# Self and cross attention of a decoder layer: values on packed weights, four value buffers, fewer waits and fewer written-out slots on TensorE

## The reference

```
def _L0_attn_ref(x, w_qkv, w_proj, b_proj):              # self attention
    qkv = einsum('bnc,cd->bnd', x, w_qkv).reshape(b, n, 3, H, HD).transpose(2, 0, 3, 1, 4)
    attn = softmax(einsum('bhnd,bhmd->bhnm', q * scale, k), axis=-1)
    out = einsum('bhnm,bhmd->bhnd', attn, v).transpose(0, 2, 1, 3).reshape(b, n, c)
    return einsum('bnc,cd->bnd', out, w_proj) + b_proj
x = _layernorm(x + _L0_attn_ref(x, ...))
x = _layernorm(x + _L0_xattn_ref(x, ctx_1024, ctx_1024, ...))   # same shape, keys and values of the context, causal
x = _layernorm(x + _L0_ffn_ref(x, ...))
x = _layernorm(x + _L1_attn_ref(x, ...))                 # differential attention, heads of 64
x = _layernorm(x + _L1_xattn_ref(ctx_1024, x, mask, ...))
x = _layernorm(x + _L1_ffn_ref(x, ...))                  # mixture of experts
```

## Time and profile before

| what | value |
|---|---|
| runs | 1548.01, 1548.19, 1548.48 us; median 1548.19 us |
| profiled execution | 1543.35 us, of it span 1541.6 us |
| busy share of the span | PE 96%, PEld 82%, DVE 81%, ACT 59%, POOL 45% |
| first layer's attention | 0 to 271 us: self items in a loop 42 to 120, written slots 120 to 160, cross items in a loop 160 to 250 |
| feed-forward, differential attention, latent attention, experts | 271 to 340, 340 to 930, 930 to 1435, to the end |
| TensorE's granted clock, mean | 0.992 of full speed |

### The profile page before, as it was taken

How to read it: one execution, slowest core, us unless ns; L and a number is a source line. 1 busy time by engine, 2 the same in 40 slices (tenths; PEclk the granted TensorE clock), 3 DMA queues, 4 the chain that set the end, 5 groups by cost and what they waited for, 6 DMA issues and landing times. The chain is left out here.

```text
span 1541.6 us, 79105 instructions
## 1 busy us (share of the span) xinstructions
PE 1486.4 (96%) x31480; PEld 1267.9 (82%) x31480; DVE 1251.3 (81%) x3574; ACT 911.8 (59%) x2620; POOL 692.9 (45%) x1140
## 2 busy tenths in 40 slices
PE   7999999998999999999999998999999999999796
PEld 5887888886777787787877786999999999999664
DVE  7998888687878888888878885688888888888655
ACT  5888888544555555555555554666666666666242
POOL 4789777212433333333333333344444444444347
PEclk9999999999999999999999999999999999999898
DMA  4215222112210011111111011121212121212231
GB/s 116 72 54 148 72 65 64 49 53 62 62 41 27 27 29 29 27 29 32 31 28 27 27 31 28 52 58 57 63 48 65 46 65 46 65 46 63 75 110 56
DMA packets 157679, 82.70 MB, mean 54 GB/s; under 512 B 17641, under 2 KB 153115, under 8 KB 157568
## 3 DMA queue, kind: packets, MB, share of 16 engines
q1 hardware_dynamic: 154800, 77.68, 18.2%
q0 software_dynamic: 2048, 3.15, 0.6%
q10 hardware_dynamic: 720, 0.33, 0.1%
HBM read 61.03 MB, written 21.27 MB: 53 GB/s over the span
## 5 line engine op out<-in xcount | busy, mean ns | idle before, releaser
L1527 PE MATMUL bank<-diff_xT,diff_w_score 128*32 128x128 f32 x8192 | 249.0, 273 | 3.3 <-ACT diff_keys L1647 1.8
L1527 PEld LDWEIGHTS bank<-diff_xT,diff_w_score 128*32 128x32 f32 x8192 | 220.6, 110 | 34.5 <-ACT diff_keys L1647 13.8
L2150 ACT ACTIVATE lat_prob<-bank,lat_neg_max 128x128 f32<-128x128 f32 x512 | 180.6, 367 | 75.9 <-DVE lat_neg_max L2269 75.6
L2375 POOL TENSOR_TENSOR lat_prob<-lat_prob,lat_inv_sum 128x512 f32<-128x512 f32 x128 | 133.4, 1042 | 198.1 <-DVE lat_inv_sum L2297 197.1
L1860 POOL TENSOR_TENSOR diff_prob<-diff_prob,diff_inv_sum 128x512 f32<-128x512 f32 x64 | 67.1, 1049 | 325.4 <-DVE diff_inv_sum L1762 325.4
L1647 ACT ACTIVATE diff_keys<-bank 128x512 f32<-128x512 f32 x256 | 151.7, 595 | 67.6 <-PE bank L1527 66.6
L2070 PE MATMUL bank<-lat_catT,lat_query 128*128 128x128 f32 x1024 | 138.4, 278 | 2.3 <-ACT lat_query L2161 2.1
L2039 PE MATMUL bank<-lat_catT,lat_w_score 128*128 128x128 f32 x1024 | 135.4, 275 | 0.6 <-ACT lat_catT L2142 0.6
L2059 PE MATMUL bank<-lat_w_vo,lat_ctxT 128*128 128x128 f32 x1024 | 132.6, 278 | 1.1 <-ACT lat_ctxT L2173 1.1
L2070 PEld LDWEIGHTS bank<-lat_catT,lat_query 128*128 128x128 f32 x1024 | 124.5, 192 | 4.7 <-ACT lat_query L2161 3.7
L2039 PEld LDWEIGHTS bank<-lat_catT,lat_w_score 128*128 128x128 f32 x1024 | 124.6, 192 | 1.2 <-ACT lat_catT L2142 0.8
(11 more groups left out here) (273 smaller groups left out, 3611.1 us busy)
## 6 DMA issues: line engine op xcount, KB each, us to landing
lat_c_rep<-cat SPq DMA_DIRECT2D x128, 128.0 KB, 2.6
stage<-low_y SPq DMA_DIRECT2D x64, 64.0 KB, 1.6
diff_x_rep<-stage SPq DMA_DIRECT2D x128, 32.0 KB, 1.7
lat_c_t<-cat SPq DMA_DIRECT2D x32, 128.0 KB, 2.2
exp_w<-in_L_ffn_w_dram SPq DMA_DIRECT2D x16, 256.0 KB
expert_rows<-latw_zeros SPq DMA_DIRECT2D x4, 548.0 KB, 5.9
exp_rows<-expert_rows SPq DMA_DIRECT2D x8, 274.0 KB
low_x_t<-in_x_dram SPq DMA_DIRECT2D x32, 64.0 KB, 1.9
```

The costliest lines, as they stand in the source:

```text
L1527: last = nc.tensor.matmul(ring[(k + d) % 2][at, j * P:(j + 1) * P], w_score[:, H1 * (k // 2) + HS * d + 4 * (k % 2) + j, at], xT[:, :], st ...
L2150: last = nc.scalar.activation(prob[:, q, m, :], ps_s[q][:, m * T:(m + 1) * T], ACT.Exp, bias=neg_max[:, q, m:m + 1], accum_out=row_sum[:, ...
L2375: nc.gpsimd.tensor_tensor(prob[:, q, :, :], prob[:, q, :, :], inv_sum[:, q, :, None].to_broadcast([P, 4, T]), ALU.mult)\
```

## The change

- `wv` becomes 64 columns wide: the weights of the even or odd heads lie packed. L379 then has 64 moving columns, and its result lies in 64 columns of PSUM per sequence. The clearing of `wv` and its semaphore go.
- `v_blk` gets four buffers in place of two, all of it cleared once. ScalarE copies the values of the even heads from partitions 0 to 63 and those of the odd heads from partitions 64 to 127, 64x128 each, in place of one 128x256; the zeros of the other half stay from the clearing. `v_ready` counts two per item. ScalarE no longer waits for L394 of the slot (`av_done`) before this copy.
- Seven waits of TensorE's slot go, each implied by another: `onorm_done` and `oT_ready` ahead of L394, the first of its `pT_ready`, `xT_ready` (from slot 2 on) and `pT_ready` ahead of L406, `xT_ready` (from slot 2 on) and `qT_ready` ahead of L418.
- TensorE gets its own program shape in `LowHeads`: slots -2 to 5 written out, 6 to 29 looped, 30 to 33 written out, 34 to 61 looped, 62 to 66 written out. `self.quarter` tells each slot which of the four value buffers it uses. In the differential attention TensorE writes out pairs 0 and 1, loops over 2 to 30 and writes out 31 to 33.

```diff
-        self.wv = sb("wv", [P, 2, 2, P])
+        self.wv = sb("wv", [P, 2, 2, S])
-        self.v_blk = sb("v_blk", [P, 2, 2, H0 // 2, VW])
+        self.v_blk = sb("v_blk", [P, 4, 2, H0 // 2, VW])
...
     def tensor(self, pe, between=None):
-                        last = nc.tensor.matmul(ps_v[L * n:L * (n + 1), b * P:(b + 1) * P],
+                        last = nc.tensor.matmul(ps_v[L * n:L * (n + 1), b * S:(b + 1) * S],
                                                 self.xT[:, par, int(cr(0)), at:at + L], self.wv[:, int(cr(0)), odd, :],
                                                 start=True, stop=True)
...
-                wait(pe, self.onorm_done, i - 2)
-                wait(pe, self.oT_ready, i - 2)
...
-                    if hp % 4 == 0:
+                    if hp == 4 or hp == 0 and not on(0):
                         wait(pe, self.pT_ready, 2 * i - 3 + hp // 4)
...
-                wait(pe, self.xT_ready, i + 2)
-                wait(pe, self.pT_ready, 2 * i - 2)
+                if isinstance(i, int) and i < 2:
+                    wait(pe, self.xT_ready, i + 2)
...
-                wait(pe, self.xT_ready, i + 2)
-                wait(pe, self.qT_ready, i + 1)
+                if isinstance(i, int) and i < 2:
+                    wait(pe, self.xT_ready, i + 2)
...
-                wait(pe, self.v_ready, i + 1 if on(0) else NI)
+                wait(pe, self.v_ready, 2 * i + 2 if on(0) else 2 * NI)
...
-        self.slots(pe, slot, between)
+        for i in range(-2, 6):
+            written(i)
+        with pe.Fori(1, NPAIR // 4 - 1) as q:
+            for m in range(4):
+                self.quarter = (m + 2) % 4
+                slot(4 * q + m + 2, 2 * q + m // 2 + 1, m % 2, lambda d: True, lambda d: False)
+        for i in range(NPAIR - 2, NPAIR + 2):
+            written(i)
+        with pe.Fori(NPAIR // 4, NI // 4 - 1) as q:
+            for m in range(4):
+                self.quarter = (m + 2) % 4
+                slot(4 * q + m + 2, 2 * q + m // 2 + 1, m % 2, lambda d: True, lambda d: True)
+        for i in range(NI - 2, NI + 3):
+            written(i)
+            between(i)
...
     def scalar(self, act, between=None):
                 wait(act, self.v_done, i + 2)
-                wait(act, self.av_done, i)
...
-                nc.scalar.activation(self.v_blk[:, 1 - par, :, :, 0:2 * HD0],
-                                     ps_v[:, 0:2 * P].rearrange("p (b g e) -> p b g e", b=2, e=2 * HD0),
-                                     ACT.Copy).then_inc(self.v_ready, 1)
+                for odd in range(2):
+                    at = slice(odd * S, (odd + 1) * S)
+                    nc.scalar.activation(self.v_blk[at, (self.quarter + 1) % 4, :, :, odd * HD0:(odd + 1) * HD0],
+                                         ps_v[at, 0:P].rearrange("p (b g e) -> p b g e", b=2, e=HD0),
+                                         ACT.Copy).then_inc(self.v_ready, 1)
...
     def vector(self, dve, between=None):
-        nc.vector.memset(self.wv[:, :, :, :], 0.0).then_inc(self.wv_zeroed, 1)
         both = self.v_blk[:, :, :, :, :].rearrange("p n b g e -> p (n b g) e")
-        nc.vector.memset(both[:, :, 2 * HD0:VW], 0.0).then_inc(self.ones_done, 1)
+        nc.vector.memset(both, 0.0).then_inc(self.ones_done, 1)
...
-            pairs(pe, pair)
+            for i in range(2):
+                pair(i)
+            with pe.Fori(2, NPAIR - 1) as i:
+                pair(i)
+            for i in range(NPAIR - 1, NPAIR + 2):
+                pair(i)
```

More of the change, by code:

```diff
@@ L262, in written @@
         def written(i):
+            self.quarter = i % 4
             slot(i, i // 2, i % 2, lambda d: 0 <= i + d < NI, lambda d: i + d >= NPAIR)
@@ L270, in slots @@
             for m in range(4):
+                self.quarter = m
                 slot(4 * q + m, 2 * q + m // 2, m % 2, lambda d: True, lambda d: False)
@@ L393, in slot @@
                         at = slice(L * n, L * (n + 1))
[L394 removed]
+                        last = nc.tensor.matmul(ps_o[at, hp, :], self.probT[:, hp, at], self.v_blk[:, (self.quarter + 2) % 4, n // 2, hp, :],
                                                 start=True, stop=True)
@@ L440, in slot, with written @@
                 cross_weights()
+        def written(i):
+            self.quarter = i % 4
+            slot(i, i // 2, i % 2, lambda d: 0 <= i + d < NI, lambda d: i + d >= NPAIR)
         pe.wait_ge(self.consts.ident_done, 1)
-        self.slots(pe, slot, between)
+        for i in range(-2, 6):
[13 more added lines that the diff above has]
+            between(i)
     def scalar(self, act, between=None):
```

7 lines of the change are left out of this document (2 added, 5 removed).

## The result

The changed kernel takes 1539.71 us (median; 1537.22 to 1541.24) against 1548.19 for the kernel before, now over more runs (1545.61 to 1550.3). The ratio is 0.9942, with an interval of 0.9931 to 0.9952: 7.4 to 10.7 us off. The forecast was 1541.7 us, 6.5 us off. The profiled execution takes 1537.97 us where that of before took 1543.35, so the two profiles differ by 5.4 us only. The medians differ by 3.1 us more than the profiles; that, too, has to be explained.

What follows compares the result with a forecast made beforehand. TensorE was taken to bound the first layer's loops, VectorE close behind in the self loop. Cross loop 5.3 plus self loop 1.2 gave 6.5 us off, 1548.19 to 1541.7 us; range 1538.5 to 1546.0.

Steps and rivals of the forecast that it cites:

- The value matmuls: First layer's L379: 64 columns in place of 128 shorten the segment from 0.46 to 0.24 us, saving 0.22 per slot.
- rival D: Value matmuls don't shorten as said, issue or weight loads setting their pace; 0.06 us per slot or less; chance 0.07.
- The cross loop: First layer's cross-attention slots, about 24: TensorE is the bound, so all 0.22 us per slot counts, 5.3 us saved.
- The self loop: First layer's 20 self-attention slots: VectorE's 3.62 us floor leaves 0.06 per slot, also after back edges; 1.2 us saved.
- ScalarE's copies: Copy into v_blk in two: 0.34 us in place of 0.28, bounds 0 to +0.28 more, covered by 0.35 idle.
- The waits at nothing: Seven implied TensorE waits removed: issued under running matmuls, so costed at nothing; at most 0.1 us per slot more.
- the loops' shape at nothing within 1 us: TensorE's new looped and written slots and pairs: taken as zero, from -1 to +1 us.
- Rival E: Slower: loop bodies don't stay in TensorE's instruction store, or jumps stall the ring; 1554.7 us at 1.0 per back edge; chance 0.08.
- From profile to median: Whole kernel: the median's 4.8 us above the profiled execution carried over unchanged, from 1536.9 to 1541.7 us.
- B: TensorE gives more: L394 shrinks too, by 0.1 us, cross period 3.69; 1537.5 to 1540.7 us; chance 0.16.
- C: Another ring of VectorE, ScalarE and TensorE takes most of the gain; 1543.7 to 1547.5 us; chance 0.14.
- A: The forecast itself: 4.5 to 7.5 us saved, cross loop 3.79 us a slot, 1540.7 to 1543.7 us; chance 0.55.

Runs made afterwards that it cites:

- e6: Kernel before with the values part and the seven TensorE waits gone, TensorE's program shape as before: 1550.3 us, 1.0001 of the kernel before.
- e12: Changed kernel with only the differential attention's TensorE program shape turned back (pairs 0 to 3 and 30 to 33 written out): 1540.88 us, 0.9947 of the kernel before.

## Why the prediction was right, and where only its sum was

The time, 1539.71 us, lies in the range and 2.0 us below the forecast. By its steps:

*The value matmuls: right.* 0.24 us was forecast for the segment, 0.25 was measured; it is the same with the values alone. 16 matmuls in 0.25 us are 15.6 ns each. The rule of the Trainium skill, "TensorE: Matmul & The Clock Gate", Back-to-back issue gap, that matmuls start no closer than about 25 ns, thus doesn't hold here, where they lie in four column groups, and rival D falls.

*The cross loop: right.* 0.22 us per slot over 22 slots, 4.84 us; the kernels with the values all lie between 83.71 and 84.23 us there, but for the one with a stop of 1.54 us in that stretch (e6, 86.61). Forecast for 24 slots: 5.3.

*The self loop: three times too high.* Forecast 1.2 us, measured: five groups of four slots at 14.78 against 14.85 us give 0.35. The plain slots shrank as forecast, to VectorE's floor. The step that failed is "because the jump is common to both": the idle time after a back edge was read as partly TensorE's, because the trace named L394. It stays at 0.28 though L394 is now over before the statistics end, so it doesn't wait for TensorE; it is VectorE's own, as the forecast's lower bound for those slots had it (nothing gained there). Besides, the slot that holds it grew: 14.85 - 3 x 3.68 = 3.81 us before, 14.78 - 3 x 3.60 = 3.98 after. VectorE's waits from 42 to 120 us, after the change, show where the rest went, with 0.2 us in the second row before:

```profile
DVE low_inv_sum L567 <- DVE low_stats L594: 1.2, 4, 0.3
DVE low_o_norm L575 <- DVE low_inv_sum L567: 1.2, 5, 0.4
```

The 1.0 us more over five groups is 0.2 each, about the slot's growth of 0.17. What makes VectorE wait for its own reciprocal there wasn't tried.

*ScalarE's copies: wrong, and covered.* Forecast 0.34, with bounds up to 0.56; measured 0.59, above the upper bound. The row taken, a 128x128 copy at 0.17, was the wrong one: a copy of 64 partitions is not cheaper than one of 128 with twice the columns (0.28). It fits, because the 0.35 idle plus the old copy's 0.28 make 0.63. The floor worked out for ScalarE was wrong as well: with the measured copies it gives 4.01 - 0.35 + 0.31 = 3.97 us, and the slot runs at 3.80, so not everything between two waits was work that can't move closer. ScalarE is now busy 79.36 of 85 us in the cross stretch, as VectorE is (79.67), and the two are next in line.

*The waits at nothing, the loops' shape at nothing within 1 us: wrong as rules, right in their sum here.* Alone the removed waits cost 5.7 us, and with the other parts in place they gained some 3. Alone the shapes gave nothing, and with values and waits they gave 9. What was missing is a cost that the profile of before doesn't show at all: TensorE stops of up to 2.3 us where the program passes through code that is fetched, at a packet's edge. Written slots hold such places, and 21 fewer packets mean fewer of them. Rival E looked at the right resource but on the wrong side: back edges, a second pass of code that is already there, cost TensorE next to nothing (the cross loop's slot with a back edge takes 3.83 against 3.80 us), while first passes, exits and written code can. The Trainium skill, "Runtime: NRT & Kernel Launch", Instruction fetch mechanics, says that the crossing from one 16 KiB block to the next is mostly hidden, and that a jump to code outside the window stalls. The first agrees with the traces as far as most crossings show nothing; but those that show, in rows of neighbours 256 instructions apart, stand in written slots and the first pass of the loop behind them (slots 4 to 8, 30 to 33 and 32 to 36), with no jump back in between, and took up to 2.29 us. No run here shows the second.

*From profile to median: the step that made the sum right by luck.* I took the 4.8 us between the profile of before and its median over to the changed kernel unchanged. It isn't constant: after the change it is 1.7 us. The first profile of before was an execution without stops, the second (2.5 us of stops, 1547.42 us) is close to the median. Between the first profiles 5.4 us went: 4.84 in the cross loop, 0.34 in the self slots, the rest in stages that vary by more: the profile after lost 3.6 us in the slots 28 to 38, half of that to the clock, and won 1.1 us in pairs 0 to 5 and 2.0 us in "rest", where its clock was a little higher (0.91 against 0.90 from the same point to the end). The other 3.1 us of the medians' 8.5 are the difference of those two distances. That they are stops that the new shape avoids fits e6 and e12 (8 us for the first layer's shape, in that combination) and the pads. It isn't shown: only the profiled executions can be searched for stops, and the clock varies between executions by as much.

*The rivals.* The time lies where B was priced, at 1537.5 to 1540.7, but B's mechanism is absent: L394 didn't shorten. C is absent too, since the cross period came as forecast. A holds as a mechanism in the cross loop; what the time lies below it comes from elsewhere, from the distance between profile and median.

**Open.** That the stops stand at every 256th instruction is counted; that TensorE waits there for a late packet is inferred, since no trace row joins a packet to a stop. Why the same crossing costs nothing in one place or execution and 2 us in another isn't shown: most packets, all 77 of the first profile of before among them, cause no long stop. Open too is what makes the granted clock fall more often in one execution than in another.

## What to carry to other kernels

Price a shorter segment against the floor of each other engine, stage by stage; that gave the 4.84 us to a few per cent. When a trace names another engine for the idle time at a loop's back edge, as it did here, check whether the waiting engine was itself just coming round. Where an engine runs long written-out code, an edit that only adds or removes instructions can move the time by 0.3 to 0.4% either way, without any work on the path: test such an edit with a pad of half a packet and of a whole one before you believe in its gain or loss, and take the profile's distance to its median from more than one profile. Before you explain the difference of two profiles in a stage, compare the granted clock of that stage: 1 to 4 us of what first looked like the change or like chance was that. And before you call a wait that ends in "issue" a fetch, look at whether it stands between two matmuls where the code has no wait, or ahead of a run for which another engine has just finished.

## What the runs showed of the hardware

- TensorE stopped for up to 2.29 us between two matmuls of one run, where the code has no wait, in written code, in a loop's first pass and behind its exit, and in fourteen profiles never in the stretches of later passes from 60 to 115, 185 to 240 and 440 to 840 us. Neighbouring stops lie 254 to 258 of TensorE's instructions apart (ten distances, one of them 512 for two), and the 32 added matmuls, 128 instructions with their weight loads, moved the stop of slot 4 by 64 matmuls. 127 added instructions moved the whole kernel from 1.0037 to 0.9993 in one version and from 0.9942 to 0.997 in another; 255 left the latter at 0.9947.
- Two ScalarE copies of 64x128 from PSUM took 0.59 us, where one of 128x256 took 0.28.
- 16 matmuls of 64 columns in four column groups took 0.25 us, 15.6 ns each.
- The same code from slot 64 to pair 0 took 77.90 us at a granted clock of 1.00, 79.28 to 79.94 at 0.98, and 80.64 to 81.09 at 0.96.
- VectorE's step over a back edge takes 0.57 us (89.19 to 89.76), against 0.33 without one (81.86 to 82.19).
